# A causal mask moved from VectorE to TensorE, and a convolution's left products moved to GpSimd

## What is computed

```python
x = x + tanh(g_xattn[n]) * xattn_n(layernorm(x), ctx)
x = x + tanh(g_ffn[n])   * ffn_n(layernorm(x))
```

```python
h = bit_linear(x, w1)                  # 256 -> 1024
h = depthwise_conv1d(h, conv_w, conv_b)  # three taps over the tokens
h = silu(h)
return bit_linear(h, w2)               # 1024 -> 256
```

```python
a = einsum('bhqd,bhkd->bhqk', q, k) * hd ** -0.5
a = softmax(where(triu(ones, 1), -1e9, a))
```

## Time and profile before

| | |
|---|---|
| median of 3 runs | 2839.97 us (2837.9 to 2842.7) |
| the profiled execution | 2830.95 us, span 2829.7 us |
| TensorE busy | 2597.7 us, 92% of the span |
| VectorE busy | 2187.3 us, 77% |
| ScalarE busy | 1684.6 us, 60% |
| GpSimd busy | 1134.9 us, 40% |
| mean granted clock of TensorE | 0.975 of full speed |

### The profile page before, as it was taken

How to read it: one execution, slowest core, us unless ns; L and a number is a source line. 1 busy time by engine, 2 the same in 40 slices (tenths; PEclk the granted TensorE clock), 3 DMA queues, 4 the chain that set the end, 5 groups by cost and what they waited for, 6 DMA issues and landing times.

```text
span 2829.7 us, 60900 instructions
## 1 busy us (share of the span) xinstructions
PE 2597.7 (92%) x23748; PEld 2122.2 (75%) x23748; DVE 2187.3 (77%) x4794; ACT 1684.6 (60%) x4539; POOL 1134.9 (40%) x1981
## 2 busy tenths in 40 slices
PE   7797989899888989999899999999999999999999
PEld 5676767677666767777777777888787878788777
DVE  7868697877678587786767777787878787778998
ACT  4565666666555666666555555655656565656544
POOL 2132323323443543324454444333333333435676
PEclk9898999999899999999999999999999999999999
DMA  6000000000011121100012121100000000000110
GB/s 189 3 24 9 18 13 18 14 13 18 11 48 40 63 77 42 30 16 24 11 46 62 55 76 58 33 19 20 21 16 21 16 24 13 24 3 25 33 36 21
DMA packets 84168, 92.15 MB, mean 33 GB/s; under 512 B 15332, under 2 KB 77288, under 8 KB 83880
## 3 DMA queue, kind: packets, MB, share of 16 engines
q1 hardware_dynamic: 75432, 59.91, 6.9%
q0 software_dynamic: 8448, 28.34, 3.4%
HBM read 65.36 MB, written 22.85 MB: 31 GB/s over the span
## 4 chain that ended last, share of the span: by engine, by line
PE 63%; DVE 23%; ACT 5%; POOL 4%; issue 3%; DMA 1%; SPq 1%; DVEq 0%; POOLq 0%; ACTq 0%
PE psum L353 14%; PE psum L377 12%; PE psum L346 12%; PE psum L403 6%; DVE tiny L730 4%; PE psum L415 3%; PE psum L532 3%; DVE big L738 3%; PE psum L370 3%; PE psum L360 3%; PE psum L367 2%; PE psum L526 2%; PE psum L513 2%; DVE xn L711 1%; DVE tiny L766 1%
## 5 line engine op out<-in xcount | busy, mean ns | idle before, releaser
L377 PE MATMUL psum<-ident,big 128*128 128x128 f32 x2784 | 428.2, 285 | 66.2 <-ACT big L1219 22.4
L377 PEld LDWEIGHTS psum<-ident,big 128*128 128x128 f32 x2784 | 324.0, 145 | 140.2 <-ACT big L1219 49.3
L1219 ACT ACTIVATE big<-big 128x512 f32<-128x512 f32 x512 | 312.1, 631 | 170.4 <-DVE big L738 168.5
L730 DVE TENSOR_REDUCE tiny<-psum 128x8 f32<-128x1024 f32 x256 | 312.3, 1220 | 47.5 <-PE psum L403 42.8
L738 DVE TENSOR_TENSOR big<-psum,tiny 128x512 f32<-128x512 f32 x512 | 329.6, 685 | 8.8
L1382 POOL TENSOR_SCALAR tiny<-mv 128x1 f32<-128x1 f32 x224 | 53.0, 236 | 677.1 <-DVE mv L701 674.9
L403 PE MATMUL psum<-head_keys,small 64*128 64x256 f32 x2048 | 285.9, 403 | 19.7 <-ACT big L1226 10.9
L1399 POOL TENSOR_TENSOR head_keys<-big,head_rows 128x512 f32<-128x512 f32 x256 | 266.6, 1060 | 0.0
L1424 POOL TENSOR_TENSOR big<-big,tiny 128x512 f32<-128x512 f32 x128 | 133.8, 1052 | 308.2 <-DVE tiny L773 308.0
L403 PEld LDWEIGHTS psum<-head_keys,small 64*128 64x128 f32 x2048 | 185.3, 189 | 74.6 <-issue 56.9
L1263 ACT ACTIVATE big<-psum,tiny 128x128 f32<-128x128 f32 x512 | 181.7, 382 | 38.1 <-DVE tiny L768 37.6
(11 more groups left out here) (334 smaller groups left out, 6616.7 us busy)
## 6 DMA issues: line engine op xcount, KB each, us to landing
ctxT<-in_ctxT SPq DMA_DIRECT2D x64, 128.0 KB, 2.2
after_L_xattn<-x SPq DMA_DIRECT2D x64, 128.0 KB, 1.7
mixture_out<-spare SPq DMA_DIRECT2D x46, 128.0 KB, 1.7
x_in<-in_x SPq DMA_DIRECT2D x32, 128.0 KB, 2.2
mixture_in<-xn SPq DMA_DIRECT2D x32, 128.0 KB, 1.7
x_in<-after_L_xattn SPq DMA_DIRECT2D x32, 128.0 KB, 2.1
w_bits<-after_L_xattn SPq DMA_DIRECT2D x32, 128.0 KB, 2.1
spare<-in_L_w SPq DMA_DIRECT2D x2, 1024.0 KB, 7.2
```

The source lines that it names most:

```text
L377: last = pe.transpose(bank[:, k * P:(k + 1) * P], src[:, k * P:(k + 1) * P], identity)
L730: dve.tensor_reduce(top, s8, AX.X, ALU.max).then_inc(*t.dve.tell(p, f"{l}.top{r}"))
L1219: last = act.activation(flat, flat, ACT.Exp, scale=DH ** -0.5)
```

## The change

First, the mask. VectorE's minimum is gone. In the opening VectorE makes a bfloat16 tile `m.future` of 128 x 512, four times the mask with 0 on and below the diagonal and -4e9 above. In each round of `self` TensorE multiplies it with the bfloat16 identity into each of the two banks (`start=True`), and the scores are accumulated on top.

Second, the convolution. `pool_conv` is new: GpSimd multiplies each half of the hidden features with the left tap's weights into `t.head_keys[half]` (signals `lp0`, `lp1`). VectorE adds the result with one instruction where it had four.

Third, all five strings of `ORDER` are written anew. Each lane has as many turns on each engine as before, except for two more on GpSimd in each of the 8 passes of the first half.

```diff
-SPREAD = {"L2": "clip", "self": "mask"}
+SPREAD = {"L2": "clip"}
...
-        "pool": NORM["pool"],
+        "pool": NORM["pool"] + " lp0 lp1",
...
 ORDER = {
     "pe": (
-        "3231314231212111323213121121213234230231023113100222200033331111313121323210301301030101131030200123"
+        "4212312134321302202110313022312102012331201313003032022200111121212100203032332121121022302322021132"
...
         else:
             pe.wait_ge(*t.act.at(p, f"{l}.eT1"))
+        if l == "self":
+            for half in range(2):
+                pe.matmul(t.ab[:, half, :], m.ident_bf[:], m.future[:].rearrange("p h s -> p (h s)"), start=True, stop=False)
         keys = t.head_keys[r].rearrange("p h s -> p (h s)")
         for cols in (slice(0, D), slice(D, 2 * D)):
             for half in range(2):
                 rows = slice(half * P // 2, (half + 1) * P // 2)
-                last = pe.matmul(t.ab[:, half, cols], t.qT[rows, r, :], keys[rows, cols], start=True, stop=True)
+                last = pe.matmul(t.ab[:, half, cols], t.qT[rows, r, :], keys[rows, cols],
+                                 start=l != "self", stop=l != "self" or cols.start > 0)
...
-        if l == "self":
-            dve.tensor_tensor(s8, s8, m.causal[:].rearrange("p (o s) -> p o s", o=1).to_broadcast([P, 2 * CH, S]),
-                              ALU.min).then_inc(*t.dve.tell(p, f"{l}.mask{r}"))
-            dve.wait_ge(*t.dve.at(p, f"{l}.mask{r}"))
...
         dve.wait_ge(*t.act.at(p, f"{l}.cen{half}"))
-        for k in ks:
-            last = dve.scalar_tensor_tensor(t.act_h[:, k, 1:S], t.hid[:, k, 0:S - 1], m.w["conv"][:, k, 0:1],
-                                            t.act_h[:, k, 1:S], ALU.mult, ALU.add)
-        then(last, f"left{half}")
+        dve.wait_ge(*t.pool.at(p, f"{l}.lp{half}"))
+        then(dve.tensor_tensor(t.act_h[:, ks[0]:ks[-1] + 1, 1:S], t.act_h[:, ks[0]:ks[-1] + 1, 1:S],
+                               t.head_keys[half][:, :, 0:S - 1], ALU.add), f"left{half}")
...
+    dve.tensor_scalar(m.future[:], m.causal[:].rearrange("p (o s) -> p o s", o=1).to_broadcast([P, CH, S]), 0.0, None, ALU.min)
...
+def pool_conv(pool, m, t, p, l):
+
+    for half in range(2):
+        sl = slice(4 * half, 4 * half + 4)
+        pool.wait_ge(*t.dve.at(p, f"{l}.hid{half}"))
+        pool.tensor_tensor(t.head_keys[half][:, :, 0:S - 1], t.hid[:, sl, 0:S - 1],
+                           m.w["conv"][:, sl, 0:1].to_broadcast([P, 4, S - 1]), ALU.mult
+                           ).then_inc(*t.pool.tell(p, f"{l}.lp{half}"))
+        yield
...
         yield from pool_rstd(pool, m, t, p, "bit")
+        yield from pool_conv(pool, m, t, p, "bit")
...
+    m.future = sb("future", [P, CH, S], BF16)
```

More of the change, by code:

```diff
@@ new lines @@
+        "1031313223022013103011132032031101201310102303201211012300303030033212322212212313000203121323132102"
+        "1233103321121021203102320230123213102320320201302202312013103131332012301012031230110312012013010233"
+        "0300313121130022033203202012331230313102031200212331332212113210231013201223123031013122103210312312"
+        "3120133012202201100103110321210210231230303112013103203003033200203321320102033021030323032111331323"
+        "2121231311123020010213223310201312212032012310132102102123320112030122022110010131012312100211331130"
@@ new lines @@
+        "2023210202130310203013310012201231001033020212013010133100100323132313320201233123301021020210210320"
+        "1231231201302231031230131221320211020321230123113212022103310113103220003030320310210323120023023100"
+        "3123130101032021203302320021031032131323131031023212023302311032102012020223123131031202310312310212"
+        "3213210202130103212322130131313032002111133203203220320310103020321320030223302203201033001231230130"
+        "0302211331331021021121003202301130213130220310123102020213021320231331103010232221131210221331203032"
@@ new lines @@
+        "2012312312123102022110132300301123313010203201320130321031122312123213313121231212133231113231231310"
+        "3103002130313221020301112230020121030213013213210200133013023321221113231032230211032203232120023110"
+        "1132312201030203032101303231023230320210130203332232001330130221231302102302301323211201230300112121"
+        "0331221200101221310010201023031321203120320113012313212213121032320321031013202301202132002301311320"
+        "0230113012120133013020133103203123032303212002122032333100312210313020120120301213132310231230230021"
@@ new lines @@
+        "3231032213100201310202102103021230321303003110132301212213102013301202303230323121100313202310202011"
+        "0130320231101201330130130231013120020321323003203022103302031221213231230230131030120231132100210331"
+        "2210012030212301032321032002110331301212233213101320313022023010111322320231020203031320120123301132"
+        "0313013012100230123123300230102210332031223003232123123103100023113201230020113221201031221020302132"
+        "0312310100330321122233132303112230130121301322032210011102332100301210221033021131303120130102223010"
@@ new lines @@
+        "3220233301323013330210100312101022320201031323303210113102132020120203213323032212101311201300100201"
+        "03113312303332a919a03a39a391a018978a79a089780a7938a79a08097837909a9a7a8907a793a808007978a8793ab8acb9"
+        "7c8b978abc0bc789ab89bca780b7a89a9c7a9bc8b07c8a7bcabc07ba65c6c57c8786856c5bc68b57c8675b6c58976c95aba6"
+        "bc56985cb86c65b65bac58c6bc6b5b76597b9657b6c9ac56ba58c98659c65aca59a6c659659858685675b76ab5ca7cb76a7b"
+        "6cbc56cb5b6b956c98c68965c68b5967b96575b9a6587ac58ba5c78b657ac6ba95986785bc65bc69a757b56c758"
@@ L257 @@
+        "94b7a46b5a985647a4b564"
     ),
     "pool": (
[L259 to L262 removed]
```

179 lines of the change are left out of this document (77 added, 102 removed).

## The result

The changed kernel took 2847.19 us (median of 17 runs, 2843.92 to 2849.49) against 2838.34 us for the kernel before on the same chips (17 runs, 2834.41 to 2843.67). The ratio is 1.0028, 95% interval 1.0022 to 1.0035: 0.28% slower, about +8 us, where 0.6% faster was forecast. The profiled execution of after lies at its median; that of before (2830.95) lay 7.4 us under the median measured here, so the two spans differ by more (16.3 us) than the runs do.

The account below looks back on a forecast made before the run. TensorE, busy 92% of the span, was taken to have least room in the second stretch; -27.4 - 0.5 + 18.4 + 0.7 - 10.6 + 3.0 = -16.4 us gave 2824 us, 0.6% faster, range 2788 to 2860.

Parts of the forecast that it names:

- rival (2): First half: additions on the chain wait out GpSimd's second product, giving back the convolution's gain; +3.7 us, 2844 us, chance 0.15.
- mask off VectorE: Self attention, second half: removing 64 VectorE masks gives -27.4 us on the chain and -0.5 for issue steps.
- mask's matmuls, with the tile: Self attention: 128 matmuls take 28.5 us of TensorE, +18.4 reaching the end; making the mask tile in the opening, +0.7.
- convolution: four products to one addition: First half: 22 groups of VectorE left products on the chain, 25.6 us, become additions of 15.0 us; -10.6 us.
- GpSimd products: First half: 64 products, 67 us on GpSimd, slow VectorE by 8.8 us, of which +3.0 us on the chain.
- new order: All engines: new orders spend the shorter waits by moving pieces closer; taken as 0, with 15 us allowed either way.
- On the chain they give -27.4 us: Second stretch: VectorE's masks make 2.0% of the chain, about 22 of 64, and removal returns all that time.
- rival (1): TensorE is the bound, its queue right behind, so all 28.5 us of mask matmuls are paid; +21.6, 2862 us, chance 0.27.
- VectorE's relief: VectorE's busy time was to fall by some 79 us in the second half and about 20 in the first.
- the queue of GpSimd has room: First half: GpSimd's waits for VectorE's statistics total 674.9 us, so products holding its queue were costed at nothing.
- TensorE's idle time in the second stretch: Sign of the forecast being right: TensorE's idle in the second half falls from 64 to about 26 us.
- Rival (3): VectorE was the real limit and masks off the chain count too; together -74 us, 2766 us, chance 0.08.

Follow-up runs that it names:

- nomask_old: Kernel before, in its old order, with VectorE's causal mask left out and nothing in its place: 2821.7 us, ratio 0.9969.
- maskadd_old: Kernel before, old order, with TensorE's mask matmuls added while VectorE keeps its own mask: 2853.88 us, ratio 1.0081.
- addonly_old: Kernel before, old order, VectorE's four left products replaced by the single addition, nobody making the left products: 2827.46 us, ratio 0.9981.
- conv_old: Kernel before, old order, with only the convolution's left products moved to GpSimd: 2843.65 us, ratio 1.0020.
- both_old: Kernel before, old order, with both the mask and the convolution edits: 2858.75 us, ratio 1.0083.
- mask_old: Kernel before, old order, with only the mask moved to TensorE: 2857.0 us, ratio 1.0062.
- extra_old: Kernel before, old order, GpSimd's 64 left products added and waited for but unused, VectorE keeping its own four: 2851.09 us, ratio 1.0065.
- order_only: Kernel before with the new order alone, mask and left products still on VectorE: 2911.74 us, ratio 1.0260.
- extra_tiny_old: Kernel before, old order, extra unused GpSimd products with all turns and waits, but one element per partition row: 2828.93 us, ratio 0.9991.

## Why the prediction was wrong

The sign was wrong. 2847 lies within the wide range of 2788 to 2860, and next to rival (2)'s 2844, but that is luck: rival (2)'s mechanism was not found, and the number is what misses in both directions left over. Term by term:

| step of the prediction | forecast | measured | from |
|---|---|---|---|
| mask off VectorE | -27.9 | -8.8 | nomask_old |
| mask's matmuls, with the tile | +19.1 | +22.9 | maskadd_old |
| convolution: four products to one addition | -10.6 | -5.4 | addonly_old |
| GpSimd products | +3.0 | +11.1 | conv_old less addonly_old |
| new order | 0 | -15.6 | changed kernel less both_old |
| sum | -16.4 | +4.2 | changed kernel: +8 |

The 4 us between the sum and the changed kernel are within what the intervals of five measurements allow; the mask's halves give -8.8 + 22.9 = +14.1 where mask_old has +17.6.

**The step that failed** is "On the chain they give -27.4 us". The prediction took a line's time on the chain for what its removal gives. That holds only as far as no other path is close behind. It asked what is late next on VectorE (the maximum, the subtraction) and not on TensorE, which took over the path: 8.8 of 27.9 us came back, 32%. The other terms of the sum come to +11.5, so with 8.8 in place of 27.9 the sum is +2.7 (at 11.9, the upper end of its interval, just below zero): this step alone turns it. The 77% of rival (1) as a turning point holds only where all 28.5 us are paid; at the sum's 18.4 it is 41%. TensorE's 64 us of idle time were no warning, since they are more than 27.9: nomask_old still leaves 57.

**The matmuls' step** was mis-sized. The pace was close, 0.24 against 0.223 us. The share that reaches the end was put at the chain's 64.5%; it was 22.9 / 28.5 = 80% in the old order (67 to 97% by the interval). In the new order 27.4 / 28.5 = 96% came out, of which the traces place 23.4 us, 82%, in the second half. How much of it is TensorE's time and how much the later start of the maximum was not separated. The tile took 0.97 us, above the 0.68 that was called the most. So the two mask steps erred the same way: a relief of the engine with air counted too high, a load on the engine without air too low. Rival (1) described this, and in mask_old its sign is there: the second half is 25.6 us longer (1365.7 against 1340.1) with TensorE's idle time in the stretch at 61.5 us, 64 before. Its size was too high, +29.2 for the mask where mask_old has +17.6; that both_old's +23.5 is near its +21.6 in all is chance, since it kept the convolution's gain. The Trainium skill (TensorE: Matmul & The Clock Gate, Back-to-back issue gap) would have 131 ns for one such matmul in a stream; the chain does not show that, it shows 0.24 us, and here its pairs stand between other work.

**The convolution's relief** had the same fault, half of it kept (5.4 of 10.6).

**The GpSimd products** were costed by VectorE's slowdown, 0.13 us per us of product, times the share on the chain. The slowdown is there and larger (18.2 us of VectorE's busy time in the first half of extra_old against 8.8 forecast), and its effect at the end was 18.4 us alone and 11.1 behind the relief, well above 3.0. The granted clock, 0.94 against 0.96, had no term. Rival (2) was right that the products give back the convolution's gain and wrong in how: the addition's mean is 804 ns, well above 0.68 us as it said, but its waits for GpSimd are 0.9 us in all, and 122 ns more in each of 64 additions are 8 us, not one product of 1.05 each. The share of 22 in 64 did not last either, with 43 additions on the chain. The Trainium skill (SBUF — State Buffer, SBUF: two separate sides) has VectorE with two SBUF inputs and GpSimd exclude each other. Here the left and right products take both their tiles from SBUF; that they are longer beside whole products and not beside one-element products agrees in direction. The 0.60 against 0.29 us of the earlier trace rows were the weaker support, because L839 reads one tile and a scalar. Since in conv_old the -5.4 and the products' cost come out at +5.7, the edit is a loss by itself.

**The new order** was forecast at 0 with 15 either way and brought 15.6. Without it the change would have cost 23.5 us. The prediction's reading, that shorter waits are spent by moving pieces closer, fits order_only's waits; it did not see that this makes the order worth anything only with the new operations.

**Right** were L727's disappearance, VectorE's relief (-74 and -23 against -79 and -20), TensorE's +26 against +28, and that the queue of GpSimd has room (extra_tiny_old). TensorE's waits for the scalings L1424 rose from 20.0 to 29.1 us in the changed kernel, but are 19.6 in conv_old, so the products alone did not do that. TensorE's idle time in the second stretch fell to 39 us, not 26: the second half grew longer by 7.1 us instead of shorter by 9.5. Rival (3), VectorE the real limit, is out: taking its mask away for nothing gave 8.8 us.

## What to carry to other kernels

The chain tells what set the end, not what removing it returns: before counting a line's time on it, ask which queue would take over. That engine's whole idle time is too loose a bound (64 us here, for a gain of 8.8). Nearer are those of its waits that the removed work can delay, here 24 us, and even of these 5 came back. Leave the work out altogether for one run: that prices a relief before anything is built in its place. With orders written out by hand, time an edit both in the old order and in the new, and never judge an order without the operations it was made for.

## What was not expected of the hardware

- 64 GpSimd products of 1.05 us, whose result nobody used, cost 18.4 us, and 64 of one element each, with the same waits, -2.5 (interval -5.4 to 0). For the same instructions in the first half VectorE was busy 18.2 us longer and TensorE 16.7 us longer, at a mean granted clock of 0.94 against 0.96. Placing them 1.6 us later changed nothing that could be measured.
- A bfloat16 matmul of 512 columns took 0.215 to 0.30 us of the chain in a pair, 0.24 on average.
- The same operations in another order cost 2.6%, nine times the effect of the whole change.
